# A two-layer transformer kernel with sparse experts: the first layer's routing is cut in four and moved one step on, and its dispatch and feed-forward follow

## The chip, the cores and the metric

The kernel runs on one core of a Trainium2 chip. The metric is the device time of one execution in microseconds (us). Before the change the median of three runs is 541.39 us (540.93 to 545.23).

## The reference, cut to what matters

```python
x = L0_attn_x                                   # (8, 256, 128)
xn = layernorm(x)
x = x + attention0(xn) + experts0(xn)           # layer 0
xn = layernorm(x)
x = x + attention1(xn) + experts1(xn)           # layer 1

# attention0: 16 heads of 8, causal, softmax over 256 keys, output projection
# experts0, for each batch of 256 tokens:
probs = softmax(xn @ Wr)                        # 8 experts
p, e = top_k(probs, 2)
pos  = running count of earlier choices of the same expert in this batch
keep = pos < 40                                 # capacity int(256 / 8 * 1.25)
buf[e, b, pos] += xn * keep
y = relu(buf @ W1 + b1) @ W2 + b2               # per expert, hidden 512
out = sum over the two choices of y[e, b, pos] * keep * p
# attention1: rotary, 4 key/value heads; experts1: top 2 of 8, gelu, all tokens
```

## The kernel before, in words

Every tensor stays on the core; 2048 tokens are 16 tiles of 128, two tiles to a batch, eight batches. Attention of both layers is one software pipeline of 19 steps, t = 0 to 18, written out in order by `attention_plan` (lines 122 to 231). In step t, batch a = t has its queries and keys made (`qk`, L1420 in layer 0 and L1427/L1430 in layer 1) and sent through DRAM to be restacked by SyncE's DMA queue (`stack`); batch b = t-1 has its scores computed once for the row maxima (`nat` on PE, L1464 and L1468, then `max` on DVE, L1058); batch c = t-2 has its scores computed again with the maximum subtracted (`st` on PE, L1493), the exponential taken (`exp` on ACT, L823), the causal mask applied (`msk` on POOL, L688) and is multiplied with the values (`pv` on PE, L1512); batch d = t-3 is normalised, projected and added to the residual. A step has twelve units u = 0 to 11, with one `nat`, `st`, `max` and `exp` in each and the rest put among them. Batches 0 to 7 are layer 0, 8 to 15 layer 1. The plan is one list; each engine walks it in this order and performs the items that are its own, so the place of an item fixes its place in every engine's queue.

**Layer 0's routing** (before). In step 0, unit 3, `lg` makes all logits (32 matmuls of 8 columns into PSUM bank P0, L1401), and `route` on DVE (L1020 to L1039) copies them, takes top 2 and positions (16 `max`, 16 `max_index`), makes `sel` and `selb`, and the gates. `ones_rows(1)` and `ones_rows(2)` on ACT (L781, constant rows of the stacks of batches 1 and 2) stand at `lg`. In step 1, unit 0, `cum` (PE, L1410, waits for `selb`) and `keys` (DVE) finish the positions. `disp` (DVE, L1147), `dsm` (PE, L1555, bank M0) and `dse` (ACT, L849) gather the tokens of one batch into its expert slots; steps 1 and 2 do four batches each.

**The feed-forward** of layer 0 (`ffn`, all eight experts, L1697 to L1711) stands between step 2 and step 3, with no attention beside it. After it SyncE writes a 2.5 MB buffer of zeros and goes on with the stacks.

**Combining.** For batch g = t-3 (steps 3 to 10): `disp` again and `gm` (POOL, L698, gated one-hot) at unit 4, `gt` (PE transposes, L1566; portion 0 to bank M1, portion 1 to M0) and `gte` (ACT) at units 8 and 9. For batch e = t-4 (steps 4 to 11): `py` (PE, L1581) at unit 4, `po` (PE, L1592; DVE adds and takes moments; POOL `norm_a`) at 5, `px` at 9 (DVE makes the second layer's input, L1179; POOL `bias_out`, L714; PE transposes it, L1601; ACT copies it, L879) and `pl` at 10 (PE, L1609, layer 1's logits; POOL `norm_b`, L721 and L723; DVE `logits`, L1199 to L1209, which waits for `norm_b`). These four write bank M0 for even e and M1 for odd e.

**Banks.** `bank_uses` says which PSUM bank an item writes, and `await_free` makes PE wait until the bank's last use in the order of the plan was read. `pl` is released by `lg1_ok`, which DVE's second instruction of `logits` (L1200) raises. `qk` of layer 0 writes M1, `qk` of layer 1 writes M1 and M0 and waits for both before its first matmul.

The lines that decide about units 10 and 11 are these; POOL walks the same plan and has `msk` in each unit with u % 3 == 2, ahead of what the unit adds later:

```python
def norm_b(b):                                  # POOL, item "pl"
    pool.wait_ge(mvc_ok, b + 1)
    pool.tensor_scalar(vpe[:, s], mv2[:, s, 1], ...)
    pool.tensor_tensor(rstd2[:, s], vpe[:, s], mhalf[:, s], ALU.pow).then_inc(rstdc_ok, 1)
def logits(b):                                  # DVE, item "pl"
    await_full(dve, f"M{b % 2}", ("pl", 1, b))
    dve.wait_ge(rstdc_ok, b + 1)
```

Of the kernel before, what the change touches and what calls it, by code (L numbers as in the profile page):

```python
# [11 lines left out]
ALU = mybir.AluOpType  # L12
# [3 lines left out]
P = 128  # L16
# [102 lines left out]
FFN_AFTER, MOE_AFTER = 2, 13  # L119

def attention_plan():
# [3 lines left out]
    for t in range(2 * NB + 3):  # L126
        a, b, c, d = (divmod(x, NB) if 0 <= x < 2 * NB else None for x in (t, t - 1, t - 2, t - 3))
        g, e = (x if 0 <= x < NB else None for x in (t - 3, t - 4))
# [13 lines left out]
        for u in range(12):  # L142
# [7 lines left out]
            if t == 1 and u == 0:  # L150
                plan += [("cum",), ("keys",)]
            if t == 3 and u == 0:
                plan.append(("rcon",))
            if t in (1, 2) and u % 3 == 1:
                ffn0("disp", 4 * (t - 1) + u // 3)
# [6 lines left out]
            if t in (1, 2) and u % 3 == 2:  # L162
                ffn0("dsm", 4 * (t - 1) + u // 3)
                ffn0("dse", 4 * (t - 1) + u // 3)
# [11 lines left out]
            if u == 3:  # L176
                add("vev", a)
                add("otr", d)
                add("norm", d)
                if t == 0:  # L180
                    plan += [("lg",), ("route",)]
# [17 lines left out]
            if u == 4:  # L199
                layer1("py", e)  # L200
                ffn0("disp", g)
                ffn0("gm", g)
            if u == 5:
                add("ott", d)
                layer1("po", e)
# [39 lines left out]
def bank_uses(item):  # L245

    kind = item[0]
    if kind == "xt":
        return [("N0 N1 S0 S1".split()[item[1] % 4], item)]
    if kind == "lg":  # L250
        return [("P0", item)]
    if kind == "cum":
        return [("P1", item)]
    if kind == "rcon":
        return [("M0", item)]
    if kind == "nat":
        return [(f"N{item[3] % 2}", item)]
    if kind == "st":
        return [(f"S{(3 * item[3] + item[4]) % 2}", item)]
    if kind == "pv":  # L260
        return [(f"P{item[3] // 2}", ("o", item[1], item[2], item[3] // 2))]
    if kind == "otr":
        return [("P0", item + (0,)), ("P1", item + (1,))]
    if kind == "ott":
        return [("P0", item)]
    if kind == "proj":
        return [("P1", item)]
    if kind == "qk":
# [32 lines left out]
def build(nc, w, table, wp_d, moe_d, out):  # L301
    ctx = ExitStack()
    with ctx:
# [159 lines left out]
        def released(use):  # L463
# [10 lines left out]
            if kind in ("lg", "cum", "rcon"):  # L474
                return {"lg": (lg_ok, 1), "cum": (key_ok, 1), "rcon": (rc_ok, 1)}[kind]
# [297 lines left out]
        def _(act):  # L773
# [146 lines left out]
            def attention(plan):  # L920
                for item in plan:
# [26 lines left out]
                    if k == "route":  # L948
                        route()
# [13 lines left out]
        def _(dve):  # L963
# [56 lines left out]
            def route():  # L1020

                await_full(dve, "P0", ("lg",))
                dve.tensor_copy(lg[:].rearrange("p a e -> p (a e)"), bank["P0"][:, 0:NT * E0]).then_inc(lg_ok, 1)
                dve.wait_ge(lg_ok, 1)
                for i in range(NT):
                    last = dve.max(top[:, i, :], lg[:, i, :])
                link(last)
                for i in range(NT):
# [5 lines left out]
                dve.tensor_tensor(dlt[:], lg[:], top[:, :, 0:1].broadcast_to((P, NT, E0)), ALU.subtract)\  # L1034
                    .then_inc(exin_ok, 1)
# [296 lines left out]
            def attention(plan):  # L1332
                for at, item in enumerate(plan):
# [19 lines left out]
                    if k == "route":  # L1353
                        route()
# [26 lines left out]
        def _(pe):  # L1381
# [335 lines left out]
            def attention(plan):  # L1717
                for item in plan:
# [19 lines left out]
                    if k == "lg":  # L1738
                        router()
# [28 lines left out]
```

## Time and profile before

| | |
|---|---|
| median of 3 runs | 541.39 us |
| the profiled execution, its own time | 542.69 us |
| its span, first to last instruction | 541.0 us |
| busy: PE / DVE / ACT / POOL | 458.8 / 324.4 / 247.3 / 203.2 us |
| chain that ended last, by engine | PE 57%, POOL 16%, DVE 8%, issue 8%, DMA 5%, ACT 5% |
| mean granted TensorE clock | 0.938 |

### The profile page before, as it was taken

What the parts mean: (1) busy time and instruction counts of PE and PEld (TensorE: products, weight loads), DVE (VectorE), ACT (ScalarE), POOL (GpSimd) and SP (SyncE); (2) the same over time, 40 slices, a digit from 0 to 9 for tenths busy, and PEclk for the clock granted to TensorE, in tenths of its full rate; (3) what the DMA queues carried; (4) which work ended last, traced back from release to release, by engine and by line L of the source; (5) the groups of instructions that cost most, each with busy time, mean ns of one, the idle gap of its engine ahead of it and who ended that gap; (6) DMA issues with size and microseconds to landing.
All of it is one profiled execution on the core that took longest, in us unless ns stands there. A gap on an engine that the chain in (4) does not pass through costs nothing.

```text
span 541.0 us, 10168 instructions
## 1 busy us (share of the span) xinstructions
PE 458.8 (85%) x3431; PEld 344.6 (64%) x3431; DVE 324.4 (60%) x974; ACT 247.3 (46%) x564; POOL 203.2 (38%) x274
## 2 busy tenths in 40 slices
PE   1668899979899999989989965787999997978874
PEld 1645667656777877767656634456999995654442
DVE  5475631135777877778868964314666664564952
ACT  1821545535555564555445522323555554434542
POOL 6620110004335435435444366870000001767761
PEclk9999999989999999999999977866999998888968
DMA  5642224644314313202357120312222201322130
GB/s 157 155 123 62 71 52 119 189 116 120 94 33 122 110 37 99 76 6 79 124 113 228 46 75 28 124 44 64 60 59 80 73 23 35 107 67 81 35 90 21
DMA packets 51441, 45.89 MB, mean 85 GB/s; under 512 B 4968, under 2 KB 46464, under 8 KB 51392
## 3 DMA queue, kind: packets, MB, share of 16 engines
q1 hardware_dynamic: 47424, 35.54, 23.4%
q0 software_dynamic: 2240, 4.53, 3.1%
q10 hardware_dynamic: 1728, 5.20, 3.0%
q8 instruction: 27, 0.44, 0.3%
q14 instruction: 22, 0.18, 0.1%
HBM read 26.24 MB, written 19.01 MB: 84 GB/s over the span
## 4 chain that ended last, share of the span: by engine, by line
PE 57%; POOL 16%; DVE 8%; issue 8%; DMA 5%; ACT 5%; SPq 1%; ACTq 0%; POOLq 0%; DVEq 0%
PE ps_S L1493 6%; POOL xs L741 6%; PE ps_N L1468 5%; PE ps_N L1658 5%; PE ps_P L1512 5%; POOL PT L688 4%; PE ps_N L1464 4%; PE ps_P L1668 3%; PE ps_M L1709 3%; PE ps_M L1668 3%; PE ps_S L1658 2%; PE ps_M L1555 2%; PE ps_M L1592 2%; POOL XN L750 2%; POOL LATE L750 2%
## 5 line engine op out<-in xcount | busy, mean ns | idle before, releaser
L823 ACT ACTIVATE PT<-ps_S 128x512 f32<-128x512 f32 x192 | 112.3, 591 | 109.2 <-PE ps_S L1493 87.7
L1058 DVE TENSOR_REDUCE NM<-ps_N 128x2 f32<-128x512 f32 (+1 forms) x192 | 127.9, 682 | 51.3 <-PE ps_N L1468 40.0
L688 POOL TENSOR_SCALAR_AFFINE_SELECT PT<-PT 128x512 f32<-128x512 f32 x128 | 78.6, 639 | 172.6 <-ACT PT L823 171.9
L1468 PE MATMUL ps_N<-STK 96*128 96x256 f32 (+1 forms) x256 | 105.7, 456 | 0.0
L1493 PE MATMUL ps_S<-STK 100*128 100x128 f32 (+5 forms) x352 | 88.1, 327 | 17.1 <-ACT PT L823 13.5
L1493 PEld LDWEIGHTS ps_S<-STK 104*128 104x128 f32 (+1 forms) x352 | 62.3, 200 | 25.0 <-ACT PT L823 17.9
L1464 PE MATMUL ps_N<-maskb,identb 128*128 128x256 bf16 (+1 forms) x192 | 63.5, 331 | 11.4 <-issue 8.3
L1512 PE MATMUL ps_P<-PT,VA 128*32 128x256 f32 (+1 forms) x1024 | 59.7, 351 | 7.3 <-POOL PT L688 6.8
L1468 PEld LDWEIGHTS ps_N<-STK 96*128 96x128 f32 x256 | 53.4, 208 | 4.7 <-issue 0.7
L1512 PEld LDWEIGHTS ps_P<-PT,VA 128*32 128x32 f32 x1024 | 28.1, 114 | 36.8 <-issue 15.0
L730 POOL TENSOR_TENSOR ROT<-ROT 128x256 f32<-128x256 f32 (+1 forms) x16 | 11.3, 728 | 97.1 <-DVE ROT L1087 97.1
L1464 PEld LDWEIGHTS ps_N<-maskb,identb 128*128 128x128 bf16 x192 | 20.5, 107 | 32.1 <-issue 20.5
L915 ACT ACTIVATE LATE<-ps_N,ucol 128x128 f32<-128x128 f32 x104 | 29.5, 369 | 19.4 <-PE ps_N L1658 18.2
L741 POOL DMA_INDIRECT xs<-XN,slot x32 | 31.1, 971 | 11.6 <-issue 8.6
L1658 PE MATMUL ps_N<-LATE 128*128 128x128 f32 x208 | 30.0, 290 | 0.5 <-DVE LATE L1279 0.3
L1658 PEld LDWEIGHTS ps_N<-LATE 128*128 128x128 f32 x208 | 26.9, 202 | 1.6 <-issue 0.6
L1282 DVE COPY LATE<-EW 128x512 f32 x39 | 16.6, 426 | 13.8 <-PE ps_P L1668 8.1
L813 ACT ACTIVATE XQ<-ROT 128x256 fp32r<-128x256 f32 x8 | 3.3, 417 | 45.9 <-POOL ROT L730 45.9
L1328 DVE TENSOR_SCALAR LATE<-ps_M,consts 128x320 f32 x8 | 4.4, 551 | 33.1 <-PE ps_M L1709 33.1
L1274 DVE COPY LATE<-EW 128x512 f32 x39 | 16.7, 427 | 10.3 <-issue 4.8
L1668 PE MATMUL ps_P<-LATE 128*128 128x128 f32 x160 | 21.4, 277 | 0.0
L1110 DVE TENSOR_TENSOR MS<-ps_M,MS 8x256 fp32r<-8x256 f32 x32 | 13.1, 409 | 13.2 <-ACT MS L830 11.1
(195 smaller groups left out, 811.4 us busy)
## 6 DMA issues: line engine op xcount, KB each, us to landing
STK<-scr SPq DMA_DIRECT2D x96, 96.0 KB
scr<-XQ SPq DMA_DIRECT2D x24, 256.0 KB
ROT<-in_L_ffn_W SPq DMA_DIRECT2D x16, 256.0 KB, 3.0
EW<-in_moe ACTq DMA_DIRECT2D x8, 512.0 KB, 3.6
scr<-XQ SPq DMA_DIRECT2D x24, 128.0 KB
xs<-zero SPq DMA_DIRECT2D x1, 2496.0 KB, 11.1
LATE<-xs SPq DMA_DIRECT2D x9, 256.0 KB, 2.9
ysl<-LATE SPq DMA_DIRECT2D x9, 256.0 KB, 2.3
```

The costliest lines, as they stand in the source:

```text
L688: last = pool.affine_select(out=v, in_=v, compare_op=ALU.is_ge, fill=0.0, base=0, pattern=[[0, 4], [1, P]], channel_multiplier=-1)
L741: pool.indirect_dma_start(xs, bass.IndirectOffsetOnAxis(ap=slot[:, i, k:k + 1], axis=0), XN[:, i, :], None)\
L750: pool.indirect_dma_start(y[:, i, :], None, ysl, bass.IndirectOffsetOnAxis(ap=slot[:, i, k:k + 1], axis=0))\
L823: act.activation(PT[:, g, r, :], bank[s][:], ACT.Exp, scale=SCALE).then_inc(exp_ok, 1)
L915: act.activation(E_H[j % 2][:, P * m:P * (m + 1)], bank[UP_BANKS[j % 3]][:, P * m:P * (m + 1)], ACT.Gelu, bias=ucol[j % 2][:, m:m + 1]).th ...
L1058: dve.tensor_reduce(NM[b % 2][:, h, qt, :].rearrange("q (p c) -> q c p", p=2)[:, slots[0]:slots[-1] + 1, :], bank[s][:].rearrange("q (c p ...
L1464: mm(diag, identb[:], maskb[:, None, :].broadcast_to((P, many, P)), start=True, stop=False, skip_group_check=True)
L1468: last = mm(s[:, 2 * w_ * i:2 * w_ * (i + 1)], stk[0:QK_ROWS, c, P * qt:P * (qt + 1)], stk[0:QK_ROWS, k_slots(L, c, 2 * h, 2), 0:w_], star ...
L1493: last = mm(s[:, n * i:n * (i + m)], stk[rows, k_slots(L, c, g, 1), P * kt:P * (kt + 1)], stk[rows, c:c + m, T - n:T], start=True, stop=True)
L1512: last = mm(o, va[:, kt, head, :], pr, start=(kt == 0), stop=(kt == 1))
L1658: last = mm(o[:, P * m:P * (m + 1)], E_W1[j % 2][:, P * m:P * (m + 1)], E_XT[j % 2], start=True, stop=True)
L1668: last = mm(bank[DOWN_BANKS[j % 2]][:, 0:C], E_H[j % 2][:, P * m:P * (m + 1)], E_W2[j % 2][:, P * m:P * (m + 1)], start=(m == 0), stop=(m ...
```

## The change

`FFN_AFTER` goes from 2 to 3. The logits of layer 0 are made in four portions of four tiles (`lg`, k) at units 0, 2, 4 and 6 of step 1, in bank M0, and each is copied by DVE (`logits0`). `route` is split into `route_a` to `route_d`, at units 8 to 11 of step 1. `ones_rows(1)` and `(2)` move to the `stack` items of batches 0 and 1. `cum` and `keys` move to step 2, the slots' gathering to steps 2 and 3, `rcon` to step 4. The batch g is gone: `disp`, `gm`, `gt` and `gte` are done for batch e = t-4, `disp` and `gm` at unit 1, `gt` at 3 and 4. `py`, `po`, `px` and `pl` move to units 5, 7, 10 and 11.

```diff
-FFN_AFTER, MOE_AFTER = 2, 13
+FFN_AFTER, MOE_AFTER = 3, 13
...
-            if t == 1 and u == 0:
+            if t == 1 and u % 2 == 0 and u < 8:
+                plan.append(("lg", u // 2))
+            if t == 1 and u in (8, 9, 10, 11):
+                plan.append(("ro" + "abcd"[u - 8],))
+            if t == 2 and u == 0:
                 plan += [("cum",), ("keys",)]
-            if t == 3 and u == 0:
+            if t == 4 and u == 0:
                 plan.append(("rcon",))
-            if t in (1, 2) and u % 3 == 1:
-                ffn0("disp", 4 * (t - 1) + u // 3)
+            if t in (2, 3) and u % 3 == 1:
+                ffn0("disp", 4 * (t - 2) + u // 3)
+            if u == 1:
+                ffn0("disp", e)
+                ffn0("gm", e)
             add("nat", b, u)
             ...
-            if t in (1, 2) and u % 3 == 2:
+            if t in (2, 3) and u % 3 == 2:
...
-                if t == 0:
-                    plan += [("lg",), ("route",)]
+                ffn0("gt", e, 0)
+                ffn0("gte", e, 0)
...
             if u == 4:
-                layer1("py", e)
-                ffn0("disp", g)
-                ffn0("gm", g)
+                ffn0("gt", e, 1)
+                ffn0("gte", e, 1)
             if u == 5:
                 add("ott", d)
-                layer1("po", e)
+                layer1("py", e)
...
             if u == 7:
                 add("proj", d)
+                layer1("po", e)
             if u == 8:
                 add("res", d)
                 add("pv", c, 0)
-                ffn0("gt", g, 0)
-                ffn0("gte", g, 0)
             if u == 9:
                 add("pv", c, 1)
-                layer1("px", e)
-                ffn0("gt", g, 1)
-                ffn0("gte", g, 1)
             if u == 10:
                 add("ocp", c, 0)
-                layer1("pl", e)
+                layer1("px", e)
             if u == 11:
                 add("pv", c, 2)
+                layer1("pl", e)
...
     if kind == "lg":
-        return [("P0", item)]
+        return [("M0", item)]
...
+            def logits0(k):
+                await_full(dve, "M0", ("lg", k))
+                dve.tensor_copy(lg[:, 4 * k:4 * k + 4, :]..., bank["M0"][:, 0:4 * E0]).then_inc(lg_ok, 1)
+            def route_a():      # 16 max, dlt (its exp on ACT)
+            def route_b():      # 16 max_index
+            def route_c():      # top2, sel, selb
+            def route_d():      # zs, rz, gate
...
-                    if k == "lg":
-                        ones_rows(1)
-                        ones_rows(2)
+                    if k == "stack" and item[1] == 0 and item[2] < 2:
+                        ones_rows(item[2] + 1)
```

## Rows read from the trace of the kernel before

**Rows 1.** Table by steps: stretch, its us, busy of PE, PEld, DVE, ACT, POOL, clock, DMA, GB/s.

```profile
54.80:75.84 21.04, 18.62 (x139) 13.15 (x137) 12.90 (x26) 11.18 (x23) 4.90 (x8) 1.00 0.27 79
...
111.42:133.24 21.82, 18.58 (x161) 14.35 (x161) 12.18 (x28) 10.24 (x21) 4.88 (x7) 0.92 0.36 100
133.24:155.11 21.87, 19.31 (x182) 15.51 (x178) 14.64 (x44) 11.42 (x25) 8.72 (x15) 1.00 0.30 78
155.11:174.34 19.23, 18.66 (x178) 15.33 (x178) 14.92 (x41) 11.06 (x24) 8.62 (x15) 1.00 0.32 87
174.34:194.41 20.07, 19.02 (x178) 15.37 (x178) 15.78 (x50) 11.18 (x24) 8.62 (x15) 1.00 0.30 84
```

**Rows 2.** Instructions in time, steps 0 and 1: start us, us, engine, line, operation.

```profile
21.94 7.11 ACT L781 ACTIVATE STK<-consts 8x4096 fp32r<-8x4096 f32 x2
...
21.97 6.99 PE L1401 MATMUL ps_P<-WP,XT 128*128 128x8 f32 x32
...
29.00 0.29 DVE L1023 COPY lg<-ps_P 128x128 f32<-128x128 f32 x1 [6.40 <-PE ps_P L1401]
...
34.30 0.26 PE L1410 MATMUL ps_P<-selb,trib 128*128 128x128 bf16 x1 [3.43 <-DVE selb L1033]
...
34.43 0.61 PE L1464 MATMUL ps_N<-maskb,identb 128*128 128x512 bf16 x1
...
35.34 0.29 DVE L1039 TENSOR_TENSOR gate<-ex,rz 128x128 f32<-128x128 f32 x1
```

**Rows 3.** Instructions in time, end of step 5 to start of step 6.

```profile
169.89 0.69 DVE L1058 TENSOR_REDUCE NM<-ps_N 128x2 f32<-128x512 f32 x1 [1.09 <-PE ps_N L1468]
...
170.50 0.60 DVE L1179 TENSOR_SCALAR XN<-X,mv,rstd 128x128 f32<-128x128 f32 x2
...
171.24 0.41 PE L1601 MATMUL ps_M<-consts,XN 128*128 128x128 f32 x2 [0.35 <-DVE XN L1179]
...
172.33 0.71 POOL L723 TENSOR_TENSOR rstd<-vpe,mhalf 128x2 f32<-128x2 f32 x1
...
172.99 0.56 PE L1493 MATMUL ps_S<-STK 104*128 104x128 f32 x4
173.13 0.17 DVE L1199 TENSOR_TENSOR dlt<-mv,rc 128x16 f32<-128x16 f32 x1 [0.19 <-POOL rstd L723]
173.48 0.86 PE L1512 MATMUL ps_P<-PT,VA 128*32 128x256 f32 x16
...
173.59 0.60 ACT L823 ACTIVATE PT<-ps_S 128x512 f32<-128x512 f32 x1
...
174.26 1.22 POOL L688 TENSOR_SCALAR_AFFINE_SELECT PT<-PT 128x512 f32<-128x512 f32 x2 [1.22 <-ACT PT L823]
174.27 1.13 PE L1420 MATMUL ps_M<-XT,WP 128*128 128x256 f32 x4
```

**Rows 4.** DMA traffic from 15 to 34 us, in 40 equal slices, GB/s.

```profile
GB/s 17 0 0 112 349 339 395 354 108 0 0 168 162 181 214 147 125 192 175 179 237 137 147 226 327 325 335 328 234 27 9 24 170 261 112 71 46 12 2 1
```

**Rows 5.** Instructions in time, step 5.

```profile
157.14 0.88 DVE L1068 SCALAR_TENSOR_TENSOR XQ<-ps_M,consts,XQ 128x256 fp32r<-128x256 f32 x2 [1.33 <-ACT XQ L809]
...
158.67 0.28 PE L1464 MATMUL ps_N<-maskb,identb 128*128 128x256 bf16 x1
...
162.98 0.88 DVE L1147 TENSOR_TENSOR LATE<-consts,key 128x320 f32<-128x320 f32 x2
```

**Rows 6.** Slots' gathering matmuls: count, min/median/max ns, first and last start.

```profile
L1555 PE MATMUL ps_M<-LATE,XN x32: 432/433/871, 38.3 to 74.3; 128*128 128x320 f32 x32
```

**Rows 7.** After the feed-forward, stretches; columns of rows 1.

```profile
112.06:115.47 3.41, 1.15 (x9) 0.74 (x8) 1.19 (x5) 0.84 (x2) 0.00 (x0) 1.00 0.38 104
115.47:118.89 3.42, 3.42 (x25) 2.26 (x24) 0.89 (x3) 0.60 (x1) 0.00 (x0) 0.50 0.00 0
```

**Rows 8.** Instructions in time, steps 3 and 4, columns of rows 2.

```profile
114.81 0.36 PE L1573 MATMUL ps_M<-rwS,consts 128*128 128x8 f32 x2 [2.26 <-DVE rwB L1154]
...
136.51 0.47 PE L1493 MATMUL ps_S<-STK 100*128 100x256 f32 x2 [1.42 <-DMA STK<-scm]
```

More of the change, by code:

```diff
@@ L127, in attention_plan @@
         a, b, c, d = (divmod(x, NB) if 0 <= x < 2 * NB else None for x in (t, t - 1, t - 2, t - 3))
-        g, e = (x if 0 <= x < NB else None for x in (t - 3, t - 4))
+        e = t - 4 if 0 <= t - 4 < NB else None
         def add(kind, batch, *rest):
@@ L161, in attention_plan @@
                 add("msk", c, u // 3)
-            if t in (1, 2) and u % 3 == 2:
-                ffn0("dsm", 4 * (t - 1) + u // 3)
-                ffn0("dse", 4 * (t - 1) + u // 3)
+            if t in (2, 3) and u % 3 == 2:
+                ffn0("dsm", 4 * (t - 2) + u // 3)
+                ffn0("dse", 4 * (t - 2) + u // 3)
             if t in (10, 11) and u % 3 == 0:
@@ L473, in released @@
                 return cum_ok, 1
-            if kind in ("lg", "cum", "rcon"):
-                return {"lg": (lg_ok, 1), "cum": (key_ok, 1), "rcon": (rc_ok, 1)}[kind]
+            if kind == "lg":
+                return lg_ok, use[1] + 1
+            if kind in ("cum", "rcon"):
+                return {"cum": (key_ok, 1), "rcon": (rc_ok, 1)}[kind]
             L, b, n = use[1], use[2], seq(use[1], use[2])
@@ L947, in attention @@
                         copy_xt(item[2])
-                    if k == "route":
+                    if k == "roa":
                         route()
@@ L1018, in top2 @@
                 link(last)
[L1020 to L1024, printed above, removed]
+            def logits0(k):
+                await_full(dve, "M0", ("lg", k))
+                dve.tensor_copy(lg[:, 4 * k:4 * k + 4, :].rearrange("p a e -> p (a e)"), bank["M0"][:, 0:4 * E0]).then_inc(lg_ok, 1)
+            def route_a():
+                dve.wait_ge(lg_ok, 4)
                 for i in range(NT):
@@ L1027, in route @@
                 link(last)
+                dve.tensor_tensor(dlt[:], lg[:], top[:, :, 0:1].broadcast_to((P, NT, E0)), ALU.subtract)\
+                    .then_inc(exin_ok, 1)
+            def route_b():
                 for i in range(NT):
@@ L1033, in route @@
                 dve.tensor_copy(selb[:, 0:NT, :], sel[:]).then_inc(sel_ok, 1)
-                dve.tensor_tensor(dlt[:], lg[:], top[:, :, 0:1].broadcast_to((P, NT, E0)), ALU.subtract)\
-                    .then_inc(exin_ok, 1)
+            def route_d():
                 dve.wait_ge(ex_ok, 1)
@@ L1352, in attention @@
                         router_constants()
-                    if k == "route":
-                        route()
+                    if k == "lg":
+                        logits0(item[1])
+                    if k == "roa":
+                        route_a()
+                    if k == "rob":
+                        route_b()
+                    if k == "roc":
+                        route_c()
+                    if k == "rod":
+                        route_d()
                     if k == "r1c":
@@ L1395, in _, with router @@
             pe.wait_ge(xt0_ok, 1)
-            def router():
+            def router(k):
+                await_free(pe, "M0", ("lg", k))
                 pe.wait_ge(xt0_ok, 4)
-                for i in range(NT):
-                    last = mm(bank["P0"][:, E0 * i:E0 * (i + 1)], XT[:, P * i:P * (i + 1)], Wr, start=True, stop=True)
-                last.then_inc(full["P0"], 1)
+                for i in range(4):
+                    last = mm(M0[:, E0 * i:E0 * (i + 1)], XT[:, P * (4 * k + i):P * (4 * k + i + 1)], Wr, start=True, stop=True)
+                last.then_inc(full["M0"], 1)
             def cum():
@@ L1738, in attention @@
                     if k == "lg":
-                        router()
+                        router(item[1])
                     if k == "cum":
```

## The prediction

> **What bounds the kernel now.** The page first: PE is the busiest engine and has the largest part of the chain that ended last. Then the table by steps, to see where PE is the bound and where it isn't: in steps 5 and 6 it is busy 18.66 of 19.23 us and 19.02 of 20.07; DVE has 14.9 and 15.8 us of work there [rows 1]. So a step is PE's instructions end to end plus the waits that PE cannot fill, and whatever adds a wait on PE in each of steps 4 to 11 is paid eight times. Step 3, the first after the feed-forward, takes 21.82 us for 18.58 of PE work, step 4 takes 21.87 [rows 1]. Last the timeline of the two places that the change touches: step 0 to 1 [rows 2] and the seam between two steps [rows 3]. In the first, PE does 7 us of logits, sits idle 3.43 us for `selb`, and starts the scores only at 34.43; in the second nothing waits for long.
>
> **Part 1, the front.** Without the logits and `cum` ahead of them the first scores wait for the stack of batch 0. The DMA traffic shows its reads up to about slice 25, 26.4 to 26.9 us (the 226 to 335 GB/s behind are the expert weights) [rows 4]. So `nat` 0 starts at 26.9 instead of 34.43, a lead of 7.5 us. `ones_rows(1)` ends at 25.5 (half of the 7.11 us [rows 2]), and ACT then makes batch 1's `hi` at once, instead of at 34.6 behind the routing's exponential; its stack isn't late.
>
> Most of the lead is given back inside step 1. PE: eight `nat` at the slow clock take about 6.0 us (0.86 or 0.65 each, estimated as twice the fast 0.43 and 0.33 of a unit's two or three matmuls), three logit portions of 1.75 (a quarter of 6.99 [rows 2]) 5.2, values and transposes 1.65, and 1.2 us are lost where portion 2 waits in M0 for DVE's `vev`: `nat` 7 ends at 41.0. DVE: the seventh `max` ends at 41.85; from there `route_a` to `route_d` are the 6.6 us from 29.00 to 35.63 [rows 2] less the copy and the wait for ACT, about 6.0, and four `max` of 0.69 [rows 3]: DVE is done at 50.6. PE needs `nat` 11 before `qk(2)` and gets its bank after `max` 9, at 47.1; `qk(2)` starts at 47.9 where it was 54.80, and DVE comes to `max` 0 of step 2, behind `lo` (0.88 [rows 5]) and `keys`, at 52.1. The third `nat` of step 2, which waits for that, starts at 52.8; before it was at 58.59. Step 2 before was all fast; now its first matmuls follow the gaps of step 1 and are slow for some 3 us, of which I take 1 us as exposed (bounds 0 and 3). **Step 3 starts 4.8 us before the 75.84 at which the feed-forward began.**
>
> **Part 2, steps 3 and 4.** Four gatherings of 4 x 0.33 = 1.31 us move into step 3 (5.2 us) with 0.8 of waits for `disp`, while `gt` (0.8 us) leaves; the restart after the feed-forward leaves it too. Step 3 before was 21.82, and without the restart (waits 3.0, half clock 1.7 [rows 7], a late DMA 0.8: 5.5) 16.3; now 16.3 - 0.8 + 5.2 + 0.8 = 21.6. Step 4 now holds the restart and e = 0: 20.4 (below) + 5.5 - 0.8, as PE comes later to that DMA: 25.1. Together 46.7 against 43.7, +3.0; the 1.42 us that PE waited in step 4 for the row maxima [rows 8] is already in the 43.7. The feed-forward itself, the 2.5 MB of zeros behind it and the queues of SyncE keep their order; 35.6 us stay. SyncE's `mrow` after unit 1 comes 0.9 us later in every step, since `disp` (0.88 [rows 5]) now precedes it on DVE; in steps 5 and 6 PE never waited for that data, which is the cover, so I price this at nothing (at most 0.9 a step, were it gone). **Step 5 starts 1.8 us early.** That is all that the front leaves.
>
> **Part 3, inside the steps.** `px` stands one unit later, `po` two. Before, PE had `st` 9 and `pv` 1 to do while DVE took `max` 9 and made XN, and waited 0.35 us [rows 3]. At unit 10 there is only `st` 10: from `nat` to XN is again 0.54 + 0.69 + 0.61 + DVE to PE 0.14 (169.35 to 171.24 [rows 3]), so 0.8 (the missing `pv`, 0.86 in the rows) to 0.9 more idle: +0.9 a step. `disp` at unit 1 delays `max` 1 by 0.88: `nat` 3 has 0.6 us of air in layer 0 (+0.3), none in layer 1, where `lo` stands before it too (+0.9). Even batches win 0.84: step 6 (e = 2) is 0.84 longer than step 5 [rows 1], as `gt`'s second part there waits in M0 for ACT's copy of `px`; that order is gone. `gm` (1.26 us on POOL) finds POOL idle. Steps 5 to 7: 1.2 + 0.3 + 1.2; steps 8 to 11: 1.0 + 1.8 + 1.0 + 1.8. **+8.3.**
>
> **Part 4, the seam.** This is the largest term. `pl` moves from unit 10 to 11. In POOL's queue `norm_b` so far ran before the mask of unit 11: its second instruction is at 172.33, the mask at 174.26 [rows 3]. Now it comes after it, because `msk` is put at the head of the unit and `pl` at its tail. Then: `st` 11 starts at 172.99, ACT's exponential 0.60 later, the mask 0.67 later, 1.28 for the mask, 1.07 for `norm_b`, and 0.5 until DVE's second instruction frees `pl`'s bank: 4.1 us after `st` 11 starts. PE has `st` 11, `pv` 2 and `pl` to do in this time, 172.99 to 174.27 and 0.36 more, 1.6 us [rows 3]. Who waits: in layer 0 `qk` writes M1, which is `pl`'s bank for odd e; in layer 1 it writes both banks and waits for both. So `qk` stands for 4.1 - 1.6 = **2.5 us** going into steps 6, 8, 9, 10, 11 and 12. Going into 5 and 7 (even e, layer 0) `qk` may start, but DVE has `logits` in front of `lo` and `max` 0, ends them 5.4 us after `st` 11, and `nat` 2 (3.6 us after `qk`, 158.67 [rows 5]) slips by 1.8 us. DVE's idle stretch can't be filled: its queue is in order. 6 x 2.5 + 2 x 1.8 = **+18.6** (lower bound 0, if mask and `norm_b` end ahead of PE; upper 8 x 3.4 = 27, if PE lost all of the chain but `pv`).
>
> **Sum**, against the profiled execution's own 542.69: -1.8 + 8.3 + 18.6 = +25.1, 567.8; the median is 1.3 lower, so **566.5 us**. After step 12 nothing is changed: rank, scatter and expert tiles only start later.
>
> **The rivals.**
>
> *The clock falls in the new gaps.* Before, the only half-clock stretch between 50.6 and 313 us follows a PE idle time of 2.26 us [rows 8]: 3.42 us at 0.50, the stretch ahead busy for 1.15 of 3.41 [rows 7]. The seam's gap is 2.5 us, six times, and `px`'s gap of 1.3 stands close before it. Each fall costs up to 1.7 us: +10, **577 us**. Against it: gaps of 0.8 to 1.4 us [rows 8] caused none, and matmuls go on at both sides. The Trainium skill, "TensorE: Matmul & The Clock Gate", Part 1, has the clock throttled by default and released only by activity, which by this rule speaks against the change; the rows agree that idle PE is followed by half clock.
>
> *The seam costs nothing, the rest is as said.* If PE reached `qk` late anyhow, 542.7 - 1.8 + 8.3 = 549.2, median **548**. Against: 174.26 and 174.27 [rows 3] show mask and `qk` side by side before, so an instruction chain behind the mask must reach past `qk`.
>
> *Faster.* The front keeps its whole 7.5 us: it does if step 1 ends on the stacks' DMAs and not on DVE's routing, and if `norm_b` ends before PE has finished `pv` 2. Then 542.7 - 7.5 = 535.2, median **534**. For it: PE idle 3.43 us and the 7 us of logits in the open [rows 2]. It decides at the mask of unit 11: the exponential has to end 2.5 us earlier than in rows 3.
>
> *Nothing measurable:* the front's 1.8 us against small waits, **541**.
>
> **How the numbers follow.** Seam as worked out 0.58 (its own range 555 to 573), with falls of the clock 0.14, seam free 0.08, faster 0.10, nothing 0.10. Changes under 1% (5.4 us) can't be told from none here. Slower by over 1% (above 546.8): 0.58 + 0.14 + 0.08 = 0.80, less a little for the 548 case's lower half: 0.78; same 0.12; faster 0.10. The range reaches from the seam-free case to the clock's: 547 to 577.
>
> **What would show it.** In the profile after: `nat` 0 at about 27 us; `qk` of step 2 near 48; the feed-forward's first matmul at about 92; steps 5 to 11 of 22 to 26 us where they were 19 to 22; ahead of `qk` in steps 6 and 8 to 12 an idle PE of about 2.5 us released by DVE's L1200; POOL's `norm_b` behind the mask of unit 11; PE idle 1.3 us before `px`. I am wrong if these steps keep their length, or if DVE's logits don't wait for POOL.

## The result, and the profile after

The changed kernel takes 576.75 us (median of 4 runs, 575.84 to 580.86), the kernel before in the same comparison 541.97: **ratio 1.065, interval 1.058 to 1.071**. The profiled execution has a span of 574.1 us, 33.1 more than the 541.0 of before. The forecast was 566.5 with a range to 577: the sign and the order are right, the size is 10 us short.

First the page after, busy time by engine and the granted clock in 40 slices of 14.4 us:

```profile
PE 470.0 (82%) x3431; PEld 352.0 (61%) x3431; DVE 325.5 (57%) x977; ACT 248.7 (43%) x564; POOL 203.6 (35%) x274
...
PEclk9856999998998997999797978785799999978868
```

PE is busy 11 us longer than before (458.8) with the same 3431 matmuls; the clock row shows where most of it comes from. Then the table by stretches, which answers to [rows 1]: steps 5 and 6, step 8 (the first of layer 1), and steps 5 to 11 as one stretch.

```profile
151.27:175.36 24.09, 19.45 (x180) 15.46 (x179) 15.51 (x48) 11.40 (x24) 10.26 (x18) 1.00 0.24 69
175.36:196.82 21.46, 20.12 (x177) 16.40 (x178) 14.96 (x43) 11.27 (x24) 7.00 (x11) 0.92 0.30 78
...
220.91:248.78 27.87, 22.96 (x181) 17.09 (x182) 16.80 (x50) 10.91 (x24) 10.01 (x16) 0.89 0.13 39
...
151.27:329.86 178.59, 148.72 (x1217) 110.70 (x1216) 112.99 (x334) 77.57 (x168) 67.55 (x110) 0.92 0.26 76
```

The same stretch of before, from `qk` of step 5 to `qk` of step 12:

```profile
155.04:298.65 143.61, 134.74 (x1213) 103.29 (x1209) 111.15 (x326) 75.75 (x166) 64.73 (x106) 1.00 0.33 94
```

This pair of lines carries the case. The stretch grows by 35.0 us. PE has the same instructions (a few records are missing in both), but is busy 148.72 instead of 134.74: **14.0 us are longer matmuls**, most of them slow clock. The clock stood at half for 28.0 us of this stretch (before: 0), in six pieces, and PE was busy for 24.4 of them, so slow clock accounts for up to 12.2 us. The other 1.8 are matmuls that the profile shows as longer beside a wait; e12 below has 1.0 of such growth with the clock at 1.00 throughout. PE is idle 178.59 - 148.72 = 29.9 us instead of 8.9: **21.0 us are waits**. Before it, step 5 starts 3.8 us earlier than before (151.27, was 155.04); behind it, the rest is 1.9 us longer (244.25, was 242.35). -3.8 + 35.0 + 1.9 = 33.1.

The waits in 150 to 335 us after: engine, tile and line, what released it; us in total, times, longest us.

```profile
DVE dlt L1215 <- POOL rstd L728: 21.8, 8, 2.8
...
PE ps_M L1626 <- DVE XN L1195: 8.0, 7, 1.1
...
PE ps_M L1452 <- DVE ex L1216: 6.6, 3, 2.2
...
PE ps_M L1452 <- issue: 4.5, 2, 2.2
...
PE ps_N L1489 <- DVE NM L1074: 3.4, 6, 0.8
...
PE ps_M L1445 <- DVE ex L1216: 2.2, 1, 2.2
...
PE ps_M L1545 <- DVE XQ L1084: 1.9, 2, 1.0
```

L1445 and L1452 are `qk`: six waits of 2.2 us, 13.3 in all, the two of "issue" among them. Behind them stands DVE, which stood for POOL's `rstd` 2.8 us at a time. Going into steps 5 and 7, where `qk` may start, DVE's late queue costs PE 1.0 us each time, 3.4 us after `qk` starts (L1545). The 21.0 us add up from the timelines: 13.3 at `qk`, 1.9 at L1545, 5.5 more ahead of `px` (L1626), 3.0 for maxima and 1.1 for DMAs in layer 1, less 2.4 of waits for ACT and 1.4 at the gate transposes that were there before and are gone. In time, at the seam of steps 5 and 6, which answers to [rows 3]:

```profile
171.75 0.86 PE L1537 MATMUL ps_P<-PT,VA 128*32 128x256 f32 x16
171.86 0.60 ACT L828 ACTIVATE PT<-ps_S 128x512 f32<-128x512 f32 x1 [0.36 <-PE ps_S L1518]
172.53 1.23 POOL L693 TENSOR_SCALAR_AFFINE_SELECT PT<-PT 128x512 f32<-128x512 f32 x2 [1.12 <-ACT PT L828]
172.54 0.61 PE L1634 MATMUL ps_M<-rwS,XT 128*128 128x8 f32 x4
173.84 0.19 POOL L726 TENSOR_SCALAR vpe<-mv 128x2 f32<-128x2 f32 x1
174.12 0.71 POOL L728 TENSOR_TENSOR rstd<-vpe,mhalf 128x2 f32<-128x2 f32 x1
174.92 0.18 DVE L1215 TENSOR_TENSOR dlt<-mv,rc 128x16 f32<-128x16 f32 x1 [2.76 <-POOL rstd L728]
175.13 0.17 DVE L1216 TENSOR_TENSOR ex<-ps_M,dlt 128x16 f32<-128x16 f32 x1
...
175.36 1.06 PE L1445 MATMUL ps_M<-XT,WP 128*128 128x256 f32 x2 [2.20 <-DVE ex L1216]
```

POOL's statistics (L726, L728) start when the mask of unit 11 (L693) is through, and `qk` starts 0.23 us after DVE's second instruction (L1216) does. What follows is the second part of the cost: the next 3.4 us run at half the clock, the lower level of 1.2 GHz. Half clock begins in five of the six waits at `qk`, or 0.2 us behind them, for 3.4 us the first time and 6.8 the others (the second row below has one of these); there is none at the wait into step 9, which is as long.

```profile
175.60:179.00 3.40, 3.40 (x17) 2.32 (x20) 1.43 (x9) 1.19 (x3) 0.00 (x0) 0.50 0.00 0
219.90:226.80 6.90, 5.89 (x21) 3.20 (x25) 3.74 (x15) 0.00 (x0) 1.47 (x3) 0.51 0.00 0
```

Last the front, which answers to [rows 2]:

```profile
27.31 0.58 PE L1489 MATMUL ps_N<-maskb,identb 128*128 128x512 bf16 x1 [3.22 <-DMA STK<-scr]
...
29.00 1.71 PE L1426 MATMUL ps_M<-WP,XT 128*128 128x8 f32 x8
...
43.63 0.39 PE L1489 MATMUL ps_N<-maskb,identb 128*128 128x256 bf16 x1 [1.19 <-DVE NM L1074]
...
46.53 0.40 PE L1489 MATMUL ps_N<-maskb,identb 128*128 128x256 bf16 x1 [2.08 <-DVE NM L1074]
...
47.15 1.91 PE L1445 MATMUL ps_M<-XT,WP 128*128 128x256 f32 x4
```

The scores start 7.1 us sooner, at the DMA. The end of step 1 waits twice for maxima that stand behind DVE's routing, where, in DVE's own timeline, the top-8 of all sixteen tiles is one block of 1.18 us and its indices one from 43.49 to 45.75.

### The profile page after: what moved, and what is told of

Read it like the earlier page. It is cut to its first block and busy times, and to the rows that moved or that the text cites. A ratio compares the mean times of both kernels' runs of the same rounds, so it can differ in the third digit from the quotient of the medians.

```text
span 574.1 us, 10174 instructions
## 1 busy us (share of the span) xinstructions
PE 470.0 (82%) x3431; PEld 352.0 (61%) x3431; DVE 325.5 (57%) x977; ACT 248.7 (43%) x564; POOL 203.6 (35%) x274
## 5 line engine op out<-in xcount | busy, mean ns | idle before, releaser
L693 POOL TENSOR_SCALAR_AFFINE_SELECT PT<-PT 128x512 f32<-128x512 f32 x128 | 78.9, 642 | 108.3 <-ACT PT L828 108.2
L1493 PE MATMUL ps_N<-STK 96*128 96x256 f32 (+1 forms) x256 | 110.4, 476 | 0.0
L1518 PE MATMUL ps_S<-STK 100*128 100x128 f32 (+5 forms) x352 | 90.0, 333 | 13.3 <-ACT PT L828 9.8
L1489 PE MATMUL ps_N<-maskb,identb 128*128 128x256 bf16 (+1 forms) x192 | 66.1, 344 | 15.6 <-DVE NM L1074 12.1
L1518 PEld LDWEIGHTS ps_S<-STK 104*128 104x128 f32 (+1 forms) x352 | 64.3, 206 | 21.1 <-ACT PT L828 13.6
L1537 PE MATMUL ps_P<-PT,VA 128*32 128x256 f32 (+1 forms) x1024 | 60.8, 360 | 13.4 <-POOL PT L693 13.3
L1493 PEld LDWEIGHTS ps_N<-STK 96*128 96x128 f32 x256 | 56.3, 220 | 4.8 <-issue 0.4
L920 ACT ACTIVATE LATE<-ps_N,ucol 128x128 f32<-128x128 f32 x104 | 29.6, 370 | 19.6 <-PE ps_N L1683 19.6
L703 POOL TENSOR_TENSOR LATE<-LATE,gate 128x640 f32<-128x640 f32 x8 | 10.1, 1263 | 66.0 <-DVE LATE L1163 41.9
L1683 PEld LDWEIGHTS ps_N<-LATE 128*128 128x128 f32 x208 | 26.9, 202 | 1.8 <-issue 0.9
L1298 DVE COPY LATE<-EW 128x512 f32 x39 | 16.6, 427 | 13.7 <-PE ps_P L1693 7.9
L1344 DVE TENSOR_SCALAR LATE<-ps_M,consts 128x320 f32 x8 | 4.4, 552 | 33.1 <-PE ps_M L1734 33.1
```

The lines of the kernel that those rows point to most:

```text
L693: last = pool.affine_select(out=v, in_=v, compare_op=ALU.is_ge, fill=0.0, base=0, pattern=[[0, 4], [1, P]], channel_multiplier=-1)
L920: act.activation(E_H[j % 2][:, P * m:P * (m + 1)], bank[UP_BANKS[j % 3]][:, P * m:P * (m + 1)], ACT.Gelu, bias=ucol[j % 2][:, m:m + 1]).th ...
L1489: mm(diag, identb[:], maskb[:, None, :].broadcast_to((P, many, P)), start=True, stop=False, skip_group_check=True)
L1493: last = mm(s[:, 2 * w_ * i:2 * w_ * (i + 1)], stk[0:QK_ROWS, c, P * qt:P * (qt + 1)], stk[0:QK_ROWS, k_slots(L, c, 2 * h, 2), 0:w_], star ...
L1518: last = mm(s[:, n * i:n * (i + m)], stk[rows, k_slots(L, c, g, 1), P * kt:P * (kt + 1)], stk[rows, c:c + m, T - n:T], start=True, stop=True)
L1537: last = mm(o, va[:, kt, head, :], pr, start=(kt == 0), stop=(kt == 1))
```

## The experiments

Three names are used below: the *front* is the new place of logits, routing, gathering and feed-forward, the *middle* is the order of units in steps 4 to 11, and the *seam* is the passage from a step's unit 11 to the next step's `qk`. Two theories at the start. **Seam:** `norm_b` behind the mask holds DVE, DVE holds `qk`'s bank, and the rest is small. **Clock:** the gaps matter less by their own length than by the half-clock stretches that they bring. Every run below gives its ratio to the kernel before, timed beside it. For steps 5 to 11 the table has span, PE busy, PE idle (their difference), granted clock and the time that the clock stood at half, each from one profiled execution. Three kernels with the same order in these steps (before, e2, e7) have 143.6, 143.6 and 143.8 us there, so differences of a few us are clear.

| kernel | ratio to before [95%] | steps 5-11 us | PE busy | PE idle | clock | us at half clock |
|---|---|---|---|---|---|---|
| before | | 143.6 | 134.7 | 8.9 | 1.00 | 0 |
| changed | 1.065 [1.058, 1.071] | 178.6 | 148.7 | 29.9 | 0.92 | 28.0 |
| e1, `norm_b` first | 1.033 [1.026, 1.040] | 160.3 | 139.1 | 21.2 | 0.99 | 3.4 |
| e2, front alone | 1.006 [1.002, 1.009] | 143.6 | 134.7 | 8.8 | 1.00 | 0 |
| e3, middle alone | 1.065 [1.056, 1.074] | 175.7 | 145.2 | 30.6 | 0.95 | 17.6 |
| e4, gap filled | 1.062 [1.055, 1.069] | 172.7 | 157.0 | 15.7 | 0.97 | 10.2 |
| e5, bank freed early | 1.044 [1.033, 1.055] | 169.1 | 144.6 | 24.5 | 0.95 | 17.1 |
| e6, old units | 1.014 [1.008, 1.020] | 153.4 | 142.7 | 10.7 | 0.96 | 13.7 |
| e9, `disp` in unit 2 | 1.067 [1.061, 1.073] | 172.8 | 149.5 | 23.3 | 0.92 | 27.3 |
| e12, `disp` back too | 1.002 [0.999, 1.006] | 143.5 | 135.8 | 7.7 | 1.00 | 0 |

**e1: `norm_b` at `px`.** POOL's order alone; PE's and DVE's stay as changed.

```diff
                 if item[0] == "px":
                     bias_out(item[2])
-                if item[0] == "pl":
                     norm_b(item[2])
```

> The changed kernel, but POOL runs norm_b right behind bias_out (item px, unit 10), ahead of the mask of unit 11; nothing else moves. Seam theory: the 2.5 us that PE waits ahead of qk into steps 6 and 8 to 12 and the 1.8 us behind it into 5 and 7 go (18.6 us), and most of the half-clock stretches with them (some 8 us): about 550 us, steps 8 to 11 of 22 to 23 us instead of 27. If the seam is right but the clock falls for other reasons (px's gap, the shorter units): about 558. If the seam costs nothing: 577, unchanged.

Measured 557.22 us. In the timeline of e1, the same seam:

```profile
169.58 0.71 POOL L728 TENSOR_TENSOR rstd<-vpe,mhalf 128x2 f32<-128x2 f32 x1
...
170.35 1.22 POOL L693 TENSOR_SCALAR_AFFINE_SELECT PT<-PT 128x512 f32<-128x512 f32 x2
170.36 0.61 PE L1633 MATMUL ps_M<-rwS,XT 128*128 128x8 f32 x4
171.01 0.59 DVE L1214 TENSOR_TENSOR dlt<-mv,rc 128x16 f32<-128x16 f32 x1 [1.03 <-PE ps_M L1633]
...
171.86 0.92 PE L1444 MATMUL ps_M<-XT,WP 128*128 128x256 f32 x3 [0.89 <-DVE ex L1215]
```

DVE no longer waits for POOL but for `pl` itself, 1.0 us, and `qk` for 0.9. One moved call is worth 18.3 us in steps 5 to 11: 8.7 of idle time and 9.6 of PE busy time, with 3.4 us at half clock instead of 28.0. The seam is shown, and half of its price is the clock. The 550 us expected were missed by 7, and the rival at 558 named the wrong reason for them: the clock has hardly fallen, but 12.3 us of idle time over before are left, ahead of `px` (1.15 us a step), of `qk` (0.9) and of maxima in layer 1.

One more thing stands in this trace. In each step of layer 1 PE waits 0.80 us for ACT and, after about 1 us of work, another 0.64 to 0.85 for a maximum. Only the pair of step 8 is followed by half clock (3.4 us); behind the pair of step 9, and those of steps 10 and 11, the clock stays at 1.00:

```profile
244.97 0.66 PE L1517 MATMUL ps_S<-STK 100*128 100x128 f32 x4 [0.80 <-ACT PT L827]
...
246.68 0.28 PE L1488 MATMUL ps_N<-maskb,identb 128*128 128x256 bf16 x1 [0.64 <-DVE NM L1073]
```

```profile
246.70:250.10 3.40, 3.40 (x28) 3.25 (x28) 3.25 (x10) 1.91 (x4) 1.90 (x3) 1.00 0.09 26
```

**e2 and e3: the two halves of the change, each on its own.** e2 has the new step 1 with the old units of dispatch and layer 1 (batch 0 alone keeps them early in step 4); e3 has the old step 1 and routing with the new units.

```diff
 # e2, against the changed kernel           # g = t - 3 from batch 1 on, z = batch 0 in step 4
-  u == 1: disp e, gm e                     +  u == 1: disp z, gm z
-  u == 3: gt e 0     u == 4: gt e 1        +  u == 3: gt z 0, gt z 1
-  u == 5: py   7: po   10: px   11: pl     +  u == 4: py, disp g, gm g   5: po   9: px   10: pl
                                            +  u == 8: gt g 0   9: gt g 1
```

> The change's front alone: logits in four portions, routing in step 1, gathering in steps 2 and 3, feed-forward after step 3; py, po, px, pl, and from batch 1 on disp, gm and gt, stand where they stood before the change; batch 0's disp, gm and gt are done at units 1 and 3 of step 4. Theory: step 5 starts some 3 us earlier than before the change and steps 5 to 11 are again 19 to 22 us: 537 to 540 us. Rival, the front itself makes things slower (clock, DVE's routing in the scores): over 545. Rival, the front keeps its whole 7.5 us lead: 534.

> The kernel before with the change's middle alone: routing, gathering and feed-forward stay where they were, but disp, gm and gt are done for batch e at units 1, 3 and 4 and py, po, px, pl at 5, 7, 10, 11. Theory (all of the loss is in the order of units within steps 4 to 11): about 542 + 37 = 579 us, with idle times of some 2.2 us ahead of qk. Rival, the loss comes from the shift of the feed-forward: near 542. A sum of parts holds if this and the front alone add up to the change.

Measured 543.01 and 575.57 us. The whole loss is the middle; the two ratios multiply to 1.071, with 1.065 for the change. e3 has the waits of the changed kernel (idle 30.6 and 29.9 us) but 17.6 us at half clock where that has 28.0, so the clock's part is not fixed by the waits alone. The front alone is not faster, but slower by 0.2 to 0.9%, between its theory and its rival: it is 3.3 us ahead at step 12 (295.34, was 298.65) and still 2.7 at the last gather, and loses this at the end. From the last gather on, e2 first, then the kernel before:

```profile
517.10:540.90 23.80, 14.26 (x90) 7.61 (x90) 9.56 (x24) 5.95 (x12) 5.99 (x9) 0.58 0.18 51
```

```profile
519.80:541.00 21.20, 12.36 (x100) 7.31 (x99) 9.79 (x29) 6.88 (x14) 6.24 (x9) 0.82 0.21 58
```

The same tail of thinly busy PE was granted 0.58 in the one and 0.82 in the other. All ten executions of e2 have a lower mean clock (0.903 to 0.913) than the thirteen of before timed beside them (0.913 to 0.944), so the lower clock is no accident of one profile, and e12 below loses a lead of 4.8 us at step 12 in the same way (0.57 over its last 25 us). Why the clock falls earlier in this tail was not tried.

**e4: the gap filled.** Ten bf16 matmuls of 512 columns into an idle bank, ahead of `qk` from step 5 on; nothing depends on them.

```diff
             def qk(L, b):
                 x = XT[:, T * b:T * (b + 1)]
+                n = seq(L, b)
+                if 5 <= n <= 12:
+                    await_free(pe, "N0", ("nat", *back(L, b, 1), 0))
+                    for _ in range(10):
+                        keep_clock(bank["N0"])
```

> The changed kernel with ten bf16 matmuls of 512 columns into bank N0 ahead of qk in steps 5 to 12 (work that is not used), about 2.2 us at the fast clock, so they lie in the gap in which PE waits for pl's bank. If the half-clock stretches behind the seams come from that gap and cost some 8 to 10 us: 567 us and hardly a half-clock stretch between 180 and 330 us. If the clock's falls cost nothing or have another cause: 577 or, with 2.2 us added where no gap is, up to 585.

Measured 573.64 us. Two rows: a stretch of e4 that holds a filled gap, and the filler's group in steps 5 to 11.

```profile
218.00:222.00 4.00, 4.00 (x36) 2.25 (x34) 1.08 (x5) 0.95 (x2) 2.38 (x5) 1.00 0.02 4
```

```profile
L1474 PE MATMUL ps_N<-maskb,identb 128*128 128x512 bf16 x71 | 16.6, 378 | 0.0
```

Without the 16.6 us of filler PE is busy 140.4 where the changed kernel has 148.7, 8.3 less, with 10.2 us at half clock instead of 28.0, and the steps are 5.9 shorter in this trace. So the fall of the clock has a price of its own, beside the wait. All that is left of half clock stands behind a maximum's wait in steps 8, 10 and 11, none at a filled seam. The whole kernel doesn't show the gain: 1.062 and 1.065 have overlapping intervals, and 567 us were expected. Step 4 alone, which holds the first filler, took 28.1 us instead of 24.3: 2.3 of filler, and 6.8 us at half clock behind the restart where the changed kernel has 3.4.

**e5: the bank freed before `norm_b`.** DVE's wait for POOL moved behind the instruction that reads `pl`'s bank.

```diff
-                dve.wait_ge(rstdc_ok, b + 1)
                 dve.wait_ge(mvc_ok, b + 1)
...
                 dve.wait_ge(lg1_ok, b + 1)
+                dve.wait_ge(rstdc_ok, b + 1)
```

> The changed kernel, but DVE's logits waits for norm_b only ahead of its third instruction, so that lg1_ok frees pl's bank without waiting for POOL; DVE still stands at the wait with lo, rotary and max behind it. Two theories of what the seam costs. The bank alone (PE's wait ahead of qk): its 2.2 us waits go and the time falls by some 15 us and the clock's falls, to about 552 to 556. Both paths (DVE's late queue gives nearly the same wait one or two units later, 1.8 us in layer 0, rotary late in layer 1): about 570 to 574.

Measured 568.92 us. PE's wait ahead of `qk` falls from 2.2 to 0.9, as in e1, but only half of e1's gain is there: DVE still waits for POOL (8 times, 0.9 at most) with `lo` and the first maximum behind it, and PE's wait for ACT in layer 1 is 1.4 us where e1 has 0.8. The chain had two ends, the bank and DVE's queue, and the time is close to the 570 to 574 of that theory.

**e6: py, po, px and pl back in units 4, 5, 9, 10**, both gate transposes in unit 3; `disp` and the gate mask stay early in unit 1.

```diff
-  u == 4: gt e 1                           +  u == 3: gt e 1
-  u == 5: py   7: po   10: px   11: pl     +  u == 4: py    5: po    9: px   10: pl
```

> The changed kernel with disp and gm at unit 1 and gt at unit 3 for batch e as in the change, but py, po, px and pl back at units 4, 5, 9 and 10. Theory: without the later units neither the seam nor px's longer wait is there; left are disp ahead of max 1 (0.3 us a step in layer 0, 0.9 in layer 1), the 0.84 us won in even batches, and the front's 3.3 us up to step 12: 540 to 543 us, steps 8 to 11 of 21.1 to 22.0 us. Rival, the early gt and disp carry a good part of the loss: 550 or more.

Measured 549.28 us, where the rival stood and not the theory. In layer 0 steps 5 to 7 are back at 19.6, 19.8 and 19.6. In layer 1 all four are still 23.4 to 23.8, where before had 20.3 to 22.0, and the waits for maxima there (3.0 us over the four) don't make 2 us a step. Step 8 of e6:

```profile
216.11 0.66 PE L1518 MATMUL ps_S<-STK 100*128 100x128 f32 x4 [0.80 <-ACT PT L828]
216.29 0.87 DVE L1163 TENSOR_TENSOR LATE<-consts,key 128x320 f32<-128x320 f32 x2
...
217.09 0.67 DVE L1074 TENSOR_REDUCE NM<-ps_N 128x4 f32<-128x512 f32 x1
...
217.82 0.39 PE L1489 MATMUL ps_N<-maskb,identb 128*128 128x256 bf16 x1 [0.64 <-DVE NM L1074]
```

```profile
217.80:221.20 3.40, 3.38 (x17) 3.29 (x18) 2.60 (x8) 0.60 (x1) 1.93 (x3) 0.56 0.09 27
```

PE idles 0.80 for ACT and 1 us later 0.64 for the maximum behind `disp` (L1163), and half clock begins 0.23 us into this second wait. Steps 9 to 11 have the same pair (0.64, 0.85, 0.85) and each a half-clock stretch of 3.4 us, which begins in the second wait or at most 0.3 us behind it. This led to a new theory: the early `disp` costs layer 1 a wait and a fall of the clock.

**e9: `disp` in unit 2**, behind the first two maxima, gate transposes in unit 4.

```diff
 # against e6
-  u == 1: disp e, gm e   (before nat)      +  u == 2: disp e, gm e   (at its end)
-  u == 3: gt e 0, gt e 1                   +  u == 4: gt e 0, gt e 1   (before py)
```

> The changed kernel with py, po, px, pl in their old units 4, 5, 9, 10 and both gate transposes at unit 4, and with disp and the gate mask of the batch in unit 2, behind the first two maxima of the step, where the changed kernel and the run with the old units have them in unit 1 ahead of the maxima. If the early disp is what cost the steps of layer 1 their 2 to 3 us each (it stands ahead of the maximum that natural scores wait for, PE then falls idle and its clock is lowered), steps 8 to 11 fall from 23.4 to 23.8 us to 21 to 22, the half-clock stretch in each of them goes, and the time is about 541 to 543 us. If instead the gate transposes of the same step, or the dispatch lying in the same step as py, cost it, steps stay at 23.5 and the time at 548 to 550.

Measured 575.15 us, a miss for both theories: a new wait took the place of the old. The waits of e9, whole span:

```profile
PE ps_M L1590 <- POOL LATE L702: 13.2, 8, 1.9
```

The gate transposes now stand 1.5 us a step in layer 0 and 1.9 in layer 1 for POOL's gate mask, which comes too late for them. Batch b's chain `disp`, mask, transposes, `po` in one step has too little room: early it delays the maxima, later it is late itself. The run could not judge the theory. **e11** was the same with the faster front of e7:

> The kernel with disp in unit 2 and old units, with top-8 and index taken portion by portion in the front. The front is 3.4 us shorter (scores of step 2 at 43.5 in place of 47), the rest as in the run without it: if the theory of the early disp holds, 537 to 540 us, as fast as the front alone with spread top-8; if it falls, 545 to 547.

570.08 us, ratio 1.055 [1.049, 1.060]: the same wait (13.4 us), 5 us less in all.

**e12: as e6, with `disp` and gate mask back in unit 4 of the step before** (batch 0 keeps them in unit 1 of step 4). Nothing else moves.

```diff
             if u == 1:
-                ffn0("disp", e)
-                ffn0("gm", e)
+                ffn0("disp", z)
+                ffn0("gm", z)
...
                 layer1("py", e)
+                ffn0("disp", g)
+                ffn0("gm", g)
```

> The run with the old units (py, po, px, pl at 4, 5, 9, 10, both gate transposes at unit 3), with disp and the gate mask back where the kernel before has them, in unit 4 of the step before (batch 0 alone keeps them in unit 1 of step 4). This moves nothing else, so the gate mask has most of a step before the transposes read it, which it did not have with disp in unit 2. If the early disp ahead of the maximum cost layer 1 its 2 to 3 us a step, steps 8 to 11 go from 23.4 to 23.8 us to 21 to 22 and the time is 540 to 543 us. If the gate transposes in unit 3 of the same step, ahead of py, are what costs, steps stay at 23 or more and the time is 547 to 550.

Measured 541.83 us, steps 8 to 11 at 21.55, 21.31, 21.18 and 20.98. The same place as above, in e12:

```profile
214.71 0.66 PE L1521 MATMUL ps_S<-STK 100*128 100x128 f32 x4 [0.80 <-ACT PT L831]
214.88 0.67 DVE L1077 TENSOR_REDUCE NM<-ps_N 128x4 f32<-128x512 f32 x1
...
215.62 0.28 PE L1492 MATMUL ps_N<-maskb,identb 128*128 128x256 bf16 x1
```

```profile
215.60:219.00 3.40, 3.24 (x27) 2.94 (x27) 3.23 (x10) 2.62 (x6) 1.22 (x2) 1.00 0.10 27
```

The 0.80 for ACT is still there, the 0.64 is not, and the clock stays at 1.00. e6 against e12 is the early `disp`, with its gate mask, alone: 9.9 us in steps 5 to 11, 3.0 of idle time and 6.9 of PE busy time, 13.7 us at half clock against none. In e1 the same early `disp` brought the same waits and one fall instead of four, so these 6.9 us are its price in e6 and not everywhere.

**e7, e8, e10: can anything of it be kept?** e7 is e2 with top-8 and indices of each portion taken as its logits arrive, out of the block at 41.47. e8 is the kernel before with the second gate transposes ahead of `px` in unit 9. e10 is both.

```diff
 bank["M0"][:, 0:4 * E0]).then_inc(lg_ok, 1)
+                dve.wait_ge(lg_ok, k + 1)
+                for i in range(4 * k, 4 * k + 4):
+                    last = dve.max(top[:, i, :], lg[:, i, :])
+                link(last)
+                for i in range(4 * k, 4 * k + 4):
+                    last = dve.max_index(tix[:, i, :], top[:, i, :], lg[:, i, :])
+                link(last)
```

> The front alone (as in the earlier run), with the 16 max and 16 max_index of the routing taken portion by portion, four of each right behind each copy of logits at units 0, 2, 4 and 6, so that units 8 and 9 hold only dlt. Theory that DVE's routing at the end of step 1 gives the lead back: qk of step 2 starts 2 to 3.5 us earlier than the 46.98 us of the front alone, and the time is 539 to 541 us. Rival, PE's cold matmuls or the DMAs set the end of step 1: qk of step 2 stays at 46 to 47 us and the time at 543.

```diff
 # e8 against the kernel before, and e10 against e7: unit 9
-                layer1("px", e)
                 ffn0("gt", g, 1)
                 ffn0("gte", g, 1)
+                layer1("px", e)
```

> The kernel before with gt's second portion ahead of px in unit 9 (they were the other way round), nothing of the change. Theory that the 0.84 us by which even batches' steps are longer is PE's wait for ACT's copy of px in bank M0: steps 4, 6, 8 and 10 get 0.5 to 0.8 us shorter, 538 to 540 us. Rival, px then waits for ACT's copy of gt in the same bank and nothing is won: 541.

> The front alone with top-8 and index per portion, and the second gate transposes ahead of px in unit 9. If the two gains add, each even-numbered step from 6 to 10 is 0.35 us shorter and the time is 538 us. If the first expert tiles or the tail take the lead back, it stays at 539, within 0.2% of the front with spread top-8 alone.

e7: 539.07 us, ratio 0.9948 [0.9918, 0.9977], `qk` of step 2 at 43.56 (46.98 in e2), so it was DVE's routing block that took the lead back. e8: 0.9989 [0.9955, 1.0023]; its even steps are 0.35 us shorter, less than the 0.5 to 0.8 expected: the gate transposes no longer wait for ACT's copy of `px`, but `px`'s transposes now wait for ACT's copy of the gates (1.4 us over steps 5 to 11, as much as before). e10: 537.92 us, 0.9970 [0.9938, 1.0002], which can't be told from e7 or from the kernel before; its `qk` of step 12 is 8.1 us ahead of before (290.52) and its span 6.2. **e7 alone is faster than the kernel before by more than its interval, by half a per cent.**

## Why the prediction was right, and 10 us short

**Split of the 35 us of steps 5 to 11**, by undoing one thing after the other. The share of each in the clock holds for this order of undoing only: e1 has the early `disp`'s waits with one fall, e6 with four.

| undone | us | of it PE idle | of it PE busy | us at half clock | forecast |
|---|---|---|---|---|---|
| `norm_b` behind the mask (changed to e1) | 18.3 | 8.7 | 9.6 | 28.0 to 3.4 | 18.6, all idle |
| units of py, po, px, pl, gate transposes (e1 to e6) | 6.9 | 10.5 | -3.6 | 3.4 to 13.7 | 6.3 - 2.5 |
| early `disp` (e6 to e12) | 9.9 | 3.0 | 6.9 | 13.7 to 0 | 4.5 |
| left (e12 to before) | -0.1 | -1.2 | 1.0 | 0 to 0 | |

**Where the sum was off.** Against the profiled execution it gave 567.8 us, and this took 575.84: the front kept 2.0 us more than forecast, the waits were 5.9 us less (21.0, forecast 26.9), PE's longer matmuls, nearly all slow clock, were 14.0 where the sum had none, and step 12 brought 1.9. The mechanism was right; the term that was missing is the clock's.

**Part 1, right but for one term.** `nat` 0 at 27.31 (26.9 forecast), `qk` of step 2 at 47.15 (47.9), the third `nat` of step 2 at 52.03 (52.8). Step 3 starts 6.8 us earlier, not 4.8. 0.8 us come from the earlier third `nat`, and the 1 us of exposed slow clock in step 2 was 0, its lower bound: the lead is 7.9 us at `qk` of step 2 (which before was at 55.06, not 54.80), 6.6 at the third `nat`, where 6.9 and 5.8 were forecast, and 6.8 at the step's end, so no more than 0.2 us of slow clock shows.

**Part 2, right.** From the end of step 2 to `qk` of step 5 it is 82.24 us where it was 79.20: +3.0 as forecast, with the restart after the feed-forward now in step 4 (24.3 us; 25.1 forecast). Step 5 starts 3.8 early instead of 1.8, all of it from part 1.

**Part 3, right in kind, somewhat dear.** `px` waits 1.15 us where it waited 0.35: 0.8 a step, 0.9 forecast. The early `disp` was priced at 0.9 a step of layer 1 and 0.3 of layer 0. In the changed kernel its waits are 0.64, 0.64, 0.84 and 0.85 in layer 1 and hardly any in layer 0, 3.0 us for 4.5, with one fall of the clock behind them (step 9). Once the seam is mended it costs more: 9.4 us over the four steps of layer 1 in e6 (94.40, in e12 85.02), 2.3 a step, as each of its waits then comes 1 us behind another of 0.80 and half clock stands there. The gain of the even batches, 0.84 each, was too large: the wait that goes is 0.47, and e6 gained 0.3 in step 6 (19.80, was 20.07) and lost as much in the odd steps (19.59, was 19.23).

**Part 4, right in place, for half the reason.** POOL's `norm_b` stands behind the mask, DVE's L1215 waits 2.8 us for it, and `qk` stands 2.2 us (2.5 forecast) going into steps 6 and 8 to 12, exactly the six named; into 5 and 7 PE loses 1.0 us, not 1.8. That is 15.2 us of idle time for 18.6. The 18.3 that e1 gives back agrees with 18.6 only by luck, as two errors cancel: 0.9 us a step stays in e1, since `pl` itself is late in unit 11, and the 9.6 us of longer matmuls, which the sum didn't have, make it up.

**The rival of the clock came true with the forecast**, not instead of it. It was priced at 10 us and 577, with a chance of 0.14, and left out of the sum: this is the step of the working that failed. Slow clock costs up to 12.2 us in steps 5 to 11, as a fall mostly lasted 6.8 us and not the 3.42 taken from before. That the rival's 577 meets the median of 576.75 is luck: its waits are 5.9 us too long, its 10 us of clock are 4 below the 14.0 of longer matmuls, and the rest lies in the front, in step 12 and in how the profiled executions stand to their medians. The argument against it was that gaps of 0.8 to 1.4 us caused no fall before and that matmuls go on at both sides. Both facts stand and neither bore the weight, since the new gap is 2.2 us: before, the longest wait of PE in steps 5 to 11 is 0.8 us for ACT, once in each step of layer 1, and no second one is near it. The Trainium skill, "TensorE: Matmul & The Clock Gate", Part 1, has the clock throttled unless activity releases it; the trace agrees (0.50 for 175.6 to 179.0 behind 2.20 us of idle PE, 1.00 where e4 filled it).

**The other rivals.** Seam free: false; e6, which has the old order at the seam, is close to its 548, but with the clock's falls in it. Faster: false; alone the front is 3.3 us ahead at step 12 and loses even that. Nothing measurable: false. "After step 12 nothing is changed" was short by 1.9 us: half clock follows the wait into step 12 too, and the step takes 26.3 us instead of 24.4.

## What to carry to other kernels

When an item moves by one unit in a plan that several in-order queues share, look in each queue for what it now stands behind: here one mask of 1.2 us on the least busy engine cost 18 us. About half of that was slow clock. Price a new wait on PE twice, by its length and by the slow stretch that may stand behind it; if the rows show such a stretch behind one gap, put it into the sum with a range, as the same wait isn't followed by it every time. Time won at the start has to be followed to the last row, since a thinly busy tail can give it back by its clock.

## What the hardware showed that was not expected

One idle time of 0.80 us on PE left the clock at 1.00 (before and e12, in each of the four steps of layer 1). Followed after about 1 us of work by another of 0.64 to 0.85, it was joined by 3.4 us of half clock in all four steps of e6 (0.93 over each of these steps), in three of four in e4, and in one of four in e1. So two short waits close together can bring the clock down, and do not always; what decides it, no run here separates. The same holds for the seam's wait of 2.2 us: half clock began in it or within 1 us behind it at five of six in the changed kernel, and at four of six in e3, which has the same waits. And PE, kept busy with matmuls nobody reads (e4), finished steps 5 to 11 5.9 us sooner in the profiled execution.
